# A transformer block on one core: the score steps of each head group start at 0.24 instead of 0.27 of the group's columns

## The chip, the cores and the metric

The kernel runs on one core of one Trainium2 chip. The core has TensorE (PE, matrix products), VectorE (DVE), ScalarE (ACT), GpSimd (POOL) and SyncE (SP, which here only issues DMAs). Each works through a queue of its own in order and waits on semaphores. The metric is the device time of one execution in microseconds.

## The reference

Eight sequences of 512 rows by 512 columns in float32 go through two layers, which makes 16 passes of attention and then an expert layer.

```python
x = L0_attn_x                                            # (8, 512, 512)
x = x + layernorm(attn(layernorm(x), w_qkv, w_o))        # 16 heads of 32, rotary, causal, T = 512
x = x + layernorm(ffn(layernorm(x), ...))

def attn(x, w_qkv, w_o):
    q, k, v = split(x @ w_qkv)                           # q and k rotated over all 32 columns of a head
    scores = where(causal, q @ k.T / sqrt(32), -inf)
    return (softmax(scores) @ v) @ w_o

def ffn(x, ...):
    h = x + attention(rmsnorm(x), ...)                   # 16 heads; q and k from latents of 128 columns,
                                                         # only half of each head's 32 columns is rotated
    return h + moe(rmsnorm(h), ...)                      # one shared and 7 routed experts, top 2, silu
```

## The kernel before

The program has two halves that run one after the other: `attention_layers` and `expert_layer`. The change touches only the order of work in the first.

**Cores and groups.** The attention half calls one attention pass over one sequence a core (a name of the program, not of the chip). There are 16 of them: `core_of` gives two sequences their first layer, then the same two their second, and so on. A core has four head groups of four heads each, so there are 64 groups, numbered 0 to 63; group n belongs to core n // 4. The pattern repeats every 16 groups.

**Softmax in two passes.** For group n the kernel makes the scores twice. The first time (step `S`, product at L1008, tile `score`) only to find each row's maximum: VectorE reads the scores with a mask and reduces them (`maxima`, L827). A head has three score steps: two products of 256 columns in one bank, then one of 384, then one of 512. The maxima are then transposed (step `M`, L1019), negated by ScalarE and sent by a small DMA into the stacks of q and k. The second time (step `ST`, L1031, tile `scoresT`) the maximum is subtracted inside the product, and ScalarE takes the exponential (L646). GpSimd cuts the diagonal blocks (L568) and adds column blocks up (L579, steps `A`); TensorE multiplies by V (step `PV`, L1045) and sums the rows (step `SM`, L1054).

**Rings.** `score` has 2 banks: a score step waits until VectorE has released the step two before it. `scoresT` has 2 banks, released by ScalarE. `middle` has 2 banks for everything else (projections, transposes, output products).

**What runs beside what.** During group n TensorE makes the second scores of group n, the first scores (`S`) of group n + 1, and transposes q and k of group n + 2 (step `T`, L980, just before `M`). Between these it takes projections and other products from a list: projections of q and k (`P`, L938 or L941; `KR`, L956; `KU`, L968), latents (`LAT`, L919), values (`V`, L989 or L993), and output products of the core before (`Y`, L1066). VectorE rotates q and k (L767 to L771, L787), inverts the sums in four pieces (step `I`, L840), and does the statistics of the layer norms (L741, L743, and L865 for the sum before one). GpSimd adds the rotated part (L558, L562) and takes the roots. `T` waits for that addition.

**What sets the order.** `head_group` gives each step of a group a share of the group's columns, and `merged` walks the sorted list: before a step with share s, filler steps are issued until s times all the columns of the group have gone by. `columns_of` is the weight of a step. The same list drives all engines: each engine walks it and does its own part of every step, so a step that moves on TensorE moves on VectorE, ScalarE, GpSimd and SyncE too. The score steps get their shares from one pair of numbers:

```python
steps += [(S_AT[0] + S_AT[1] * (3 * h + part), ("S", n + 1, h, part)) for h in range(GH) for part in range(3)]
```

and the second scores, which they are woven with, have their shares written out (first share of a column block, distance between heads):

```python
for j, (first, apart) in enumerate(((0.08, 0.03), (0.22, 0.04), (0.42, 0.03), (0.58, 0.03))):
    steps += [(first + apart * h, ("ST", n, j, h)) for h in range(GH)]
steps += [(share, ("PV", n, j)) for j, share in enumerate((0.37, 0.55, 0.74))]
```

Of the kernel before, what the change touches and what calls it, by code (L numbers as in the profile page):

```python
# [47 lines left out]
ST_BANKS = 2  # L48
QUARTERED = ("P", "KR", "KU", "V", "Y", "LAT")
T_AT = (0.9, 0.9, 0.9, 0.9)  # L50
S_AT = (0.27, 0.055)
WIDE = CT * FF
CHUNKS = 3 * WIDE // 512
CHUNKS_IN = {0: (0, 1), 1: (2, 3), 2: (4, 5)}
# [161 lines left out]
def head_group(n, groups):  # L216
# [6 lines left out]
    if n + 1 < groups:  # L223
        steps += [(S_AT[0] + S_AT[1] * (3 * h + part), ("S", n + 1, h, part)) for h in range(GH) for part in range(3)]
    for j, (first, apart) in enumerate(((0.08, 0.03), (0.22, 0.04), (0.42, 0.03), (0.58, 0.03))):
# [1983 lines left out]
```

How the kernel before makes its waits and increments, by code:

```python
                def load_weights():  # L404
# [3 lines left out]
                    sp.dma_start(rope2[:, :, :, :], tables[1]).then_inc(rest_in, 16)  # L408
                    sp.dma_start(ln1w[:, :], ln1_w).then_inc(rest_in, 16)
                    sp.dma_start(wlat[:, :, 0, :], kv_d.rearrange(by_c, p=P)).then_inc(rest_in, 16)
                    sp.dma_start(wlat[:, :, 1, :], q_d.rearrange(by_c, p=P)).then_inc(rest_in, 16)
                    sp.dma_start(wku[:, :], k_u).then_inc(rest_in, 16)
                    sp.dma_start(wvu[:, :], v_u).then_inc(rest_in, 16)
                    sp.dma_start(wq2[:, :, 0, :], q_u.rearrange("p (h d) -> p h d", h=NH)).then_inc(rest_in, 16)
                    sp.dma_start(wq2[:, :, 1, :], rope_q.rearrange("p (h d) -> p h d", h=NH)).then_inc(rest_in, 16)
                    sp.dma_start(wkr[:, :, :], rope_k.rearrange(by_c, p=P)).then_inc(rest_in, 16)
                    sp.dma_start(wo[:, 1], o_w.rearrange(by_c, p=P)).then_inc(rest_in, 16)
                    sp.wait_ge(consts, N_CONSTS)
# [1 line left out]
                def stack(n):  # L420
                    sp.wait_ge(high_done, 2 * (n + 1))
                    sp.wait_ge(*middle.out(("qT", n)))
                    sp.wait_ge(*middle.out(("kT", n)))
                    if n >= STACKS:
                        sp.wait_ge(st_filled, GH * TT * (n - STACKS + 1))
                    for h in range(GH):
                        for s, chosen in enumerate((slice(0, 2), slice(2, 0, -1), slice(0, 4, 3))):
```

## Time and profile before

| | |
|---|---|
| three runs | 2479.03, 2483.03, 2485.9 us; median 2483.03 |
| profiled execution | 2483.03 us, span of its instructions 2480.9 us |
| TensorE busy | 2207.7 us, 89% |
| VectorE busy | 1513.4 us, 61% |
| ScalarE busy | 1091.5 us, 44% |
| GpSimd busy | 1061.7 us, 43% |
| mean granted TensorE clock | 0.955 |

The span runs from the first instruction to the last. The attention half ends at about 1707 us. A busy share is a mean over stages; which engine is waited for differs from one kind of group to the next.

### The profile page before, as it was taken

How to read it: one execution, taken by the hardware profiler on the slowest of the kernel's cores; microseconds unless marked ns; L12 is line 12 of the kernel's file. 1: busy time of each engine (PE TensorE's matmuls, PEld its weight loads, DVE VectorE, ACT ScalarE, POOL GpSimd, SP SyncE). 2: the span in 40 equal slices, each digit the busy share in tenths (PEclk: the TensorE clock that was granted, in tenths of full speed). 3: DMA queues.
4: the chain of work that ended last, by engine and by line, in shares of the span. 5: the costliest groups of instructions: out<-in, count | busy, mean ns of one | idle time of the engine just before them, and what ended most of it. 6: DMA issues, size and time to landing. Idle time of an engine off the chain costs nothing. (4 is left out here: it accounts for less than half of the span.)

```text
span 2480.9 us, 38185 instructions
## 1 busy us (share of the span) xinstructions
PE 2207.7 (89%) x12960; PEld 1514.6 (61%) x12960; DVE 1513.4 (61%) x4196; ACT 1091.5 (44%) x2218; POOL 1061.7 (43%) x1092
## 2 busy tenths in 40 slices
PE   6898989999889999998999989896675899999984
PEld 5665555666556566564566755552454788888873
DVE  3666766656676675666757566663554556556556
ACT  1335554334545433455443345542422455555533
POOL 1455554535554445546353465543244133333312
PEclk9999999999999999999999999997787999999996
DMA  5443554434445454354554434442456588788766
GB/s 175 111 120 113 136 169 130 137 103 127 130 131 160 124 142 137 103 145 120 153 180 129 120 103 126 109 119 78 178 211 221 178 216 192 191 215 191 210 206 220
DMA packets 221918, 375.87 MB, mean 152 GB/s; under 512 B 24862, under 2 KB 95390, under 8 KB 218910
## 3 DMA queue, kind: packets, MB, share of 16 engines
q1 hardware_dynamic: 157982, 273.74, 37.6%
q0 software_dynamic: 17792, 39.99, 8.2%
q10 hardware_dynamic: 45952, 59.71, 6.7%
q8 instruction: 105, 1.72, 0.3%
q14 instruction: 87, 0.71, 0.1%
HBM read 126.88 MB, written 145.29 MB: 110 GB/s over the span
## 5 line engine op out<-in xcount | busy, mean ns | idle before, releaser
L646 ACT ACTIVATE probs<-scoresT 128x512 f32<-128x512 f32 (+3 forms) x1024 | 426.2, 437 | 513.4 <-PE scoresT L1031 499.5
L827 DVE CUSTOM_DVE_ANT_0 unused<-score,mask 128x128 bf16<-128x128 f32 (+3 forms) x1024 | 468.9, 486 | 272.0 <-PE score L1008 257.9
L1031 PE MATMUL scoresT<-stacks 97*128 97x256 f32 (+2 forms) x1024 | 421.7, 430 | 21.4 <-ACT probs L646 9.1
L1008 PE MATMUL score<-stacks 96*128 96x256 f32 (+2 forms) x1024 | 391.6, 428 | 36.5 <-DVE rowmax L827 35.6
L579 POOL TENSOR_TENSOR probs<-probs 128x1536 f32<-128x1536 f32 (+1 forms) x128 | 372.8, 2913 | 29.5 <-PE out_ps L1045 20.7
L1008 PEld LDWEIGHTS score<-stacks 96*128 96x128 f32 x1024 | 182.4, 191 | 201.7 <-issue 150.6
L840 DVE RECIPROCAL total<-total 128x128 f32<-128x128 f32 x256 | 232.6, 932 | 93.8 <-ACT whole L657 88.5
L568 POOL TENSOR_SCALAR_AFFINE_SELECT probs<-probs 128x512 f32<-128x512 f32 x256 | 164.5, 643 | 283.9 <-ACT probs L646 283.9
L1031 PEld LDWEIGHTS scoresT<-stacks 97*128 97x128 f32 x1024 | 190.5, 191 | 149.7 <-ACT probs L646 89.1
L938 PE MATMUL middle<-wqkv,XT 128*128 128x128 f32 x2048 | 268.1, 278 | 7.0 <-ACT XT L613 6.1
L1654 POOL DMA_INDIRECT h_summed<-y,goal x88 | 141.9, 1613 | 307.1 <-ACT y L1750 287.0
L938 PEld LDWEIGHTS middle<-wqkv,XT 128*128 128x128 f32 x2048 | 258.2, 194 | 17.3 <-ACT XT L613 6.6
L1066 PE MATMUL middle<-wo,outT 128*128 128x512 f32 x512 | 257.9, 598 | 0.0
L2059 PE MATMUL into<-xh,wh 128*128 128x512 f32 x480 | 202.8, 422 | 14.3 <-DVE wl L1804 7.6
L1045 PE MATMUL out_ps<-probs,V 128*32 128x512 f32 (+3 forms) x2048 | 196.3, 456 | 3.4 <-POOL probs L568 3.4
L558 POOL TENSOR_TENSOR qk<-qk,turned 128x512 f32<-128x512 f32 x64 | 81.4, 1272 | 268.5 <-DVE turned L771 268.5
L2059 PE MATMUL into<-xl,wh 128*128 128x512 f32 x480 | 193.8, 404 | 0.0
L2059 PE MATMUL into<-xh,wl 128*128 128x512 f32 x480 | 193.4, 403 | 0.0
L1966 DVE SCALAR_TENSOR_TENSOR acts<-acts,into 128x512 f32<-128x512 f32 x60 | 41.2, 687 | 179.0 <-ACT acts L1757 104.9
L767 DVE TENSOR_TENSOR qk<-middle,rope 128x512 f32<-128x512 f32 (+1 forms) x128 | 70.9, 554 | 125.6 <-PE middle L938 76.3
L562 POOL TENSOR_TENSOR qk<-qk,turned 128x256 f32<-128x256 f32 x64 | 48.3, 758 | 205.7 <-DVE turned L771 205.7
L622 ACT ACTIVATE parts<-middle 128x512 fp32r<-128x512 f32 x128 | 73.7, 596 | 140.1 <-PE middle L980 137.8
(181 smaller groups left out, 3809.5 us busy)
## 6 DMA issues: line engine op xcount, KB each, us to landing
stacks<-parts SPq DMA_DIRECT2D x768, 128.0 KB, 2.4
x_slots<-mask ACTq DMA_DIRECT2D x56, 1032.0 KB, 4.8
xr<-x_slots SPq DMA_DIRECT2D x22, 1032.0 KB
raw<-in_gates SPq DMA_DIRECT2D x24, 512.0 KB
raw<-in_ups SPq DMA_DIRECT2D x24, 512.0 KB
raw<-in_downs SPq DMA_DIRECT2D x24, 512.0 KB
normed<-in_L_attn_x SPq DMA_DIRECT2D x8, 1024.0 KB, 8.9
rows<-in_L_attn_x SPq DMA_DIRECT2D x8, 1024.0 KB, 5.7
```

The lines of the kernel that those rows point to most:

```text
L568: pool.affine_select(out=diagonal, in_=diagonal, compare_op=ALU.is_ge, fill=0.0, base=0, pattern=[[0, GH], [1, P]], channel_multiplier=-1)\
L579: pool.tensor_tensor(probs[0][:, :, P * j:T], probs[0][:, :, P * j:T], probs[j][:, :, :], ALU.add)\
L646: act.activation(probs[j][:, h, 0:width], scoresT[:, u % ST_BANKS, first:first + width], ACT.Exp, scale=SCALE).then_inc(exp_done, 1)
L827: ins = dve.tensor_tensor_reduce(unused[:, t, 0:width], score.bank(name)[:, first:first + width], mask[:, T - width:T], 1.0, MASKED, ALU.a ...
L840: dve.reciprocal(total[:, mine], total[:, mine]).then_inc(inverted, 1)
L938: ins = pe.matmul(to, tile_of(xT, c, t), wqkv[:, c, first:first + P], start=(c == 0), stop=(c == CT - 1))
L1008: ins = pe.matmul(score.bank(name)[:, first:first + width], heads[0:ROWMAX, 0, h, t * P:(t + 1) * P], heads[0:ROWMAX, 1, h, 0:width], star ...
L1031: pe.matmul(scoresT[:, u % ST_BANKS, 0:T - first], heads[0:ROWMAX + 1, 1, h, j * P:(j + 1) * P], heads[0:ROWMAX + 1, 0, h, first:T], start ...
L1045: ins = pe.matmul(out_ps[h * HD:(h + 1) * HD, P * j:T], v[:, c % 2, j, head:head + HD], probs[j][:, h, :], start=(j == 0), stop=(j == TT - 1))
L1066: ins = pe.matmul(middle.bank(name), tile_of(outT, (NG * f + c) % OUTS, t), wo[:, core_of(f)[1], c, :], start=(c == 0), stop=(c == CT - 1))
L1654: pool.indirect_dma_start(out=summed, out_offset=bass.IndirectOffsetOnAxis(ap=goal[:, k % XR, t:t + 1], axis=0), in_=y[:, k % GIVEN, t, :] ...
L2059: ins = pe.matmul(to, left, right, start=(first and n == 0), stop=(last and n == len(pairs) - 1))
```

## The change

```diff
--- before.py
+++ after.py
@@ -48,7 +48,7 @@
 ST_BANKS = 2
 QUARTERED = ("P", "KR", "KU", "V", "Y", "LAT")
 T_AT = (0.9, 0.9, 0.9, 0.9)
-S_AT = (0.27, 0.055)
+S_AT = (0.24, 0.055)
 WIDE = CT * FF
```

The first score step of a group gets the share 0.24 instead of 0.27, the last 0.845 instead of 0.875; the distance between them stays. No instruction is added, removed or changed in form. What the engines execute comes in another order in all groups but the last, which has no score steps in it.

TensorE in group 22, the third group of a first-layer core, in which the latents of the second-layer core behind it are made (L919), from the first head's score steps (L1008) to the second head's. Before:

```order
L1008 MATMUL score<-stacks1 128x256 x2
L919 MATMUL middle<-XT,wlat 128x512
L1031 MATMUL scoresT<-stacks0 128x384
L1008 MATMUL score<-stacks1 128x384
L1031 MATMUL scoresT<-stacks0 128x384
L919 MATMUL middle<-XT,wlat 128x512
L1045 MATMUL out_ps<-probs0,V 32x512 x4
L1008 MATMUL score<-stacks1 128x512
L1031 MATMUL scoresT<-stacks0 128x256
L1008 MATMUL score<-stacks1 128x256 x2
L1031 MATMUL scoresT<-stacks0 128x256
```

After:

```order
L1008 MATMUL score<-stacks1 128x256 x2
L1031 MATMUL scoresT<-stacks0 128x384
L919 MATMUL middle<-XT,wlat 128x512
L1008 MATMUL score<-stacks1 128x384
L1031 MATMUL scoresT<-stacks0 128x384 x2
L1008 MATMUL score<-stacks1 128x512
L919 MATMUL middle<-XT,wlat 128x512
L1045 MATMUL out_ps<-probs0,V 32x512 x4
L1008 MATMUL score<-stacks1 128x256 x2
L1031 MATMUL scoresT<-stacks0 128x256 x2
```

The first head's 512-column score stood behind the four products of `PV` (L1045). It now stands in front of the latent product and of these four, directly behind the second scores (L1031).

TensorE in group 21, the second group of a first-layer core, where the projections are L938. Before:

```order
L1008 MATMUL score<-stacks0 128x256 x2
L1031 MATMUL scoresT<-stacks1 128x384
L1008 MATMUL score<-stacks0 128x384
L1031 MATMUL scoresT<-stacks1 128x384
L938 MATMUL middle<-wqkv,XT 128x128 x4
L1045 MATMUL out_ps<-probs0,V 32x512 x4
L1008 MATMUL score<-stacks0 128x512
L1031 MATMUL scoresT<-stacks1 128x256
L1008 MATMUL score<-stacks0 128x256 x2
```

After:

```order
L1008 MATMUL score<-stacks0 128x256 x2
L1031 MATMUL scoresT<-stacks1 128x384
L1008 MATMUL score<-stacks0 128x384
L1031 MATMUL scoresT<-stacks1 128x384 x2
L1008 MATMUL score<-stacks0 128x512
L938 MATMUL middle<-wqkv,XT 128x128 x4
L1045 MATMUL out_ps<-probs0,V 32x512 x4
L1008 MATMUL score<-stacks0 128x256 x2
```

Here too the 512-column score of the first head moves in front of a projection and of the four products of `PV`.

TensorE at the end of group 23, a short group, in which the values are made (L993). Before:

```order
L1008 MATMUL score<-stacks0 128x512
L1045 MATMUL out_ps<-probs2,V 32x256 x4
L1008 MATMUL score<-stacks0 128x256 x2
L993 MATMUL middle<-wvu,latT 128x128
L1008 MATMUL score<-stacks0 128x384
L1008 MATMUL score<-stacks0 128x512
L980 MATMUL middle<-ident,qk 128x128 x8
L1019 MATMUL score<-ident,rowmax 16x128
```

After:

```order
L1008 MATMUL score<-stacks0 128x512
L993 MATMUL middle<-wvu,latT 128x128 x2
L1008 MATMUL score<-stacks0 128x256 x2
L1045 MATMUL out_ps<-probs2,V 32x256 x4
L1008 MATMUL score<-stacks0 128x384
L993 MATMUL middle<-wvu,latT 128x128
L1008 MATMUL score<-stacks0 128x512
L980 MATMUL middle<-ident,qk 128x128 x8
L1019 MATMUL score<-ident,rowmax 16x128
```

The last head's two 256-column scores move in front of the four products of `PV`, and its 384-column score in front of a value product. The last 512-column score keeps its place in front of the transposes of q and k (L980) and of the maxima (L1019).

## Rows read from the trace of the kernel before

**Rows 1.** Windows of busy time, attention half: stretch, length, busy per engine (instructions), clock, DMA share, GB/s.
```profile
0.00:1707.30 1707.30, 1559.99 (x10017) 1009.73 (x10017) 1084.82 (x3190) 750.53 (x1647) 824.12 (x874) 0.98 0.46 130
```

**Rows 2.** Waits of TensorE in the attention half: total, times, longest.
```profile
PE score L1008 <- DVE rowmax L827: 35.6, 41, 3.0
PE middle L980 <- POOL qk L558: 26.6, 9, 3.9
...
PE score L1019 <- DVE rowmax L827: 6.8, 6, 1.8
```

**Rows 3.** Timeline of TensorE, group 22: start, duration, engine, line, operation [idle before].
```profile
651.38 0.34 PE L1031 MATMUL scoresT<-stacks 97*128 97x384 f32 x1
651.56 1.02 PE L919 MATMUL middle<-XT,wlat 128*128 128x512 f32 x2
...
653.50 0.50 PE L1008 MATMUL score<-stacks 96*128 96x512 f32 x1
653.84 0.28 PE L1031 MATMUL scoresT<-stacks 97*128 97x256 f32 x1
```

**Rows 4.** Timeline of VectorE, first head's second maximum in groups 22 and 26.
```profile
651.99 0.42 DVE L827 CUSTOM_DVE_ANT_0 unused<-score,mask 128x256 bf16<-128x256 f32 x1
...
753.03 0.42 DVE L827 CUSTOM_DVE_ANT_0 unused<-score,mask 128x256 bf16<-128x256 f32 x1
```

**Rows 5.** Timeline of group 21 around its first output products, TensorE and VectorE.
```profile
619.31 0.37 PE L1031 MATMUL scoresT<-stacks 97*128 97x384 f32 x1
620.50 1.06 PE L1045 MATMUL out_ps<-probs,V 128*32 128x512 f32 x8
...
619.61 0.42 DVE L827 CUSTOM_DVE_ANT_0 unused<-score,mask 128x256 bf16<-128x256 f32 x1
```

**Rows 6.** Group 21: window of GpSimd's chain, then TensorE's timeline at its end.
```profile
621.69:637.25 15.56, 10.97 (x81) 8.18 (x80) 13.08 (x39) 4.65 (x11) 14.72 (x17) 1.00 0.36 136
...
637.36 0.65 PE L980 MATMUL middle<-ident,qk 128*128 128x128 f32 x4 [3.88 <-POOL qk L558]
...
638.59 2.36 PE L1054 MATMUL sum_ps<-probs,ones 128*32 128x512 f32 x16
```

**Rows 7.** Timeline of TensorE, group 28, the first head's 512-column score.
```profile
802.34 0.50 PE L1008 MATMUL score<-stacks 96*128 96x512 f32 x1 [1.19 <-DVE rowmax L827]
```

**Rows 8.** Timeline at the end of groups 23 and 29, TensorE and VectorE.
```profile
682.92 0.51 PE L1008 MATMUL score<-stacks 96*128 96x256 f32 x2
684.16 0.51 PE L1008 MATMUL score<-stacks 96*128 96x512 f32 x1 [0.33 <-DVE rowmax L827]
...
683.68 0.42 DVE L827 CUSTOM_DVE_ANT_0 unused<-score,mask 128x256 bf16<-128x256 f32 x1
...
832.53 0.68 DVE L827 CUSTOM_DVE_ANT_0 unused<-score,mask 128x512 bf16<-128x512 f32 x1
...
834.19 0.50 PE L1008 MATMUL score<-stacks 96*128 96x512 f32 x1 [0.48 <-DVE rowmax L827]
```

**Rows 9.** Timeline from group 24 to 25, TensorE and ScalarE.
```profile
714.00 0.27 PE L1019 MATMUL score<-ident,rowmax 128*16 128x128 f32 x1 [1.02 <-DVE rowmax L827]
...
714.44 1.26 PE L1054 MATMUL sum_ps<-probs,ones 128*32 128x512 f32 x16
...
718.08 0.50 PE L1031 MATMUL scoresT<-stacks 97*128 97x512 f32 x1 [0.46 <-DMA stacks<-negmax]
...
713.51 0.80 ACT L673 ACTIVATE normed<-normed,shift,rstd 128x512 f32<-128x512 f32 x1
714.37 0.27 ACT L630 ACTIVATE negmax<-score 16x128 fp32r<-16x128 f32 x1
```

**Rows 10.** Timeline of group 25, VectorE and GpSimd at the second sum.
```profile
733.12 2.08 DVE L865 TENSOR_TENSOR rows<-normed,rows 128x512 f32<-128x512 f32 x1
...
732.30 2.34 POOL L579 TENSOR_TENSOR probs<-probs 128x1024 f32<-128x1024 f32 x1
```

**Rows 11.** Window behind TensorE's wait in group 21.
```profile
637.80:641.20 3.40, 3.40 (x29) 1.33 (x28) 0.69 (x1) 1.57 (x4) 0.00 (x0) 0.51 0.08 18
```

## The prediction, on record before the changed kernel ran

> **What bounds the kernel now.** I read the windows of busy time first. The attention half, 1707.3 of 2480.9 us, has TensorE busy for 1559.99 us at a granted clock of 0.98 [rows 1]. So TensorE's queue is the bound there, and a new order of the same instructions can win only what TensorE now waits, and lose what it begins to wait. The expert half has its own order, which the edit doesn't touch. Second come TensorE's waits in the attention half: 35.6 us in 41 waits for row maxima to leave a score bank, 6.8 us for the last maxima before they are transposed, 26.6 us in 9 waits for rotated keys [rows 2]. Third, the timeline: groups 16 to 63 repeat, with period 16, the pattern of groups 0 to 15 but for the ends, and I worked each of the 16 kinds through once. Below, "group 22" stands for all of its kind.
>
> The score tile has two banks. A score step (two 256-column products, or one of 384, or one of 512 columns) may be issued when VectorE has read the step two before it. The third step of the first head (I call it the third score) therefore waits for the first score's two maxima.
>
> **The change.** No instruction is added or removed. The 12 score steps of a group move earlier by 0.03 of the group's columns, which in TensorE's queue is 0 to 1.7 us. What matters is what each is moved past.
>
> (a) *The latent groups, 8 of them (6, 10, 22, 26 and so on).* The third score moves in front of a latent product and of the four output products [order rows of group 22]. In group 22 TensorE comes to that place at 651.56; the score is now issued at 653.50 [rows 3]. The maxima that it waits for start at 651.99 and take 0.42, so they end at 652.41 [rows 4]; VectorE does them behind the rotated keys, whose place the edit leaves alone. TensorE, which waits for nothing here today, will stand from 651.56 to about 652.47, 0.9 us. Behind it nothing gives this back: the later waits of the group (for the latents' copies, for the keys) hang on TensorE's own products and move along. In group 26 the maxima end at 753.45 in the same pattern [rows 4]. 8 x 0.9 = +7.2 us.
>
> (b) *Groups 5, 21, 37, 53.* The same move, past one projection and the output products. TensorE issues the score before it at 619.31 and would be ready at 619.5; the maxima end at 619.61 + 0.42 = 620.03 [rows 5]. The stall is 0.6 us, and the output products, now at 620.50, start at about 621.4: 0.33 for the moved score and 0.6 for the wait, 0.9 us late. They release GpSimd's first addition of probabilities. GpSimd is then busy for 14.72 of 15.56 us until the keys are rotated, and TensorE waits 3.88 us for that at 637.36 [rows 6]. So this wait can take from 0.45 (if only the lag of TensorE arrives; a multiply on GpSimd now stretched beside VectorE may shrink) to 0.9 us more. I take 0.6: 4 x 0.6 = +2.4 us.
>
> (c) *Small delays.* In groups 12, 28, 44 the third score already waits 1.19 us [rows 7]; the maxima that it waits for move ahead of a rotation on VectorE and come sooner, but it stands 1.7 us sooner itself, and the next head's score then waits for maxima behind that rotation. No row gives the net; between the 1.19 us won and as much lost I take +0.2 each, since one wait takes the other's place. In groups 0, 16, 32, 48 the second head's 384-column score comes 1 us earlier and meets its bank 0.25 us too early. Together 3 x 0.2 + 4 x 0.25 = +1.6 us; below, zero for both.
>
> (d) *Groups that end on maxima.* In the eight short groups (7, 11, 23, 27 and so on) the last 512-column score waits 0.33 us beyond its weights, until the maxima that start at 683.68 and take 0.42 have ended [rows 8]. Those maxima belong to the score at 682.92, which moves in front of the output products, 0.43 us earlier; the last score, the transposed maxima and the rest of the group follow. 8 x 0.43 = -3.4 us. In groups 13, 29, 45, 61 the same wait is 0.48 us [rows 8], but VectorE first has a 512-column maximum until 832.53 + 0.68 = 833.21; with 0.64 for the two maxima behind it the bank is free at 833.85, and the last score comes at 833.91 instead of 834.19: 4 x 0.28 = -1.1 us.
>
> (e) *Costed at nothing.* In groups 8, 24, 40, 56 the last score moves in front of a projection whose statistics VectorE now does first, and the wait of 1.02 us at 714.00 goes [rows 9]. Late next is ScalarE: it copies until 714.31 before it takes the maxima at 714.37, and the product at 718.08, which needs them back by DMA, waits already (0.46 us). TensorE will wait there what it no longer waits at 714.00. If that cover is not there, 4 x 1.02 = 4.1 us are won. In group 25 VectorE is the bound over the last 13 us, and the same maxima and sums stand before the last score in either order. Two of its sums, the second taking 2.08 us beside a GpSimd addition of 2.34 us [rows 10], trade places with maxima; I take zero of -1.4 to +0.7 us each. In the other 30 or so groups the moved scores find their bank free: the order gives margins of 0.1 us and more.
>
> The Trainium skill, "SBUF — State Buffer", section on the shared port pair, says that VectorE with two SBUF inputs and GpSimd lock each other out for a whole instruction rather than sharing. The 2.08 us row, which ends after the addition has ended, agrees with it. By that rule the sum in group 25 would end when the addition ends wherever it is put, so the maxima moved in front of it would be free, and the sum of all terms would be up to 4 x 0.7 = 2.8 us lower. I don't count it, since the addition itself is released by output products that come later.
>
> **The sum.** +7.2 + 2.4 + 1.6 - 3.4 - 1.1 = +6.7 us on the profiled run, whose own time is 2483.03 us (span 2480.9 and 2.1 around it); this is also the median of the three runs, which spread over 6.9 us. I predict 2489.5 us, 0.26% slower. Within this case the terms' bounds give 2484 to 2494.
>
> **Rivals.**
> 1. *GpSimd's chain carries more.* All of (b) at its upper bound, and in groups 9, 25, 41, 57 the late output products move GpSimd's roots, ScalarE's normalised rows and so the next group's first transposes by 0.6 us. For it: GpSimd is busy 14.72 of 15.56 us [rows 6]. Against it: behind group 25 the copies of the transposes follow the sums and not the rows. 4 x 0.3 + 4 x 0.6 more: 2493 us.
> 2. *The stalls are given back.* The small reorderings win (ScalarE's ring of two banks gets a score between its second and third product of the last column block, 0.1 to 0.2 us in some 20 groups), the copies absorb (b), and half of (a) remains: 2484 us, no change that can be measured.
> 3. *Faster.* The change does what an earlier start would suggest: the 6.8 us for the last maxima go, the term (d) doubles, and the 35.6 us of waits for score banks lose a third, above all in group 25, where single waits reach 3.0 us [rows 2]. 6.8 + 4.5 + 12 less the 7.2 of (a): 16 us, 2467 us. Against it: in group 25 VectorE itself is full, and in 24 ScalarE is late next. It decides if the maxima of group 25 come a microsecond sooner.
> 4. *The clock.* After the wait of 3.88 us the granted clock is at 0.51 from 637.8 to 641.2, that is 1.2 instead of 2.4 GHz, and the sums at 638.59 take 2.36 us [rows 6, 11]; the same 16 take 1.26 at full clock [rows 9]. If the new stall of 0.9 us in the latent groups, where the clock is full now, brings it down, each costs 1.1 to 1.7 us more: 8 x 1.4 = 11, so 2500 us. Against it: waits of 1.02 and 1.19 us [rows 7, 9] stand in stretches at full clock. The Trainium skill, "TensorE: Matmul & The Clock Gate", part 1, has an idle array fall to half rate and a busy one return; by it only the long waits of (b) matter, where one more step of half clock would add some 1.7 us each, to 2496 us. The rows agree as far as they go.
>
> **Chances.** The forecast 0.45, rival 1 0.22, rival 2 0.17, rival 3 0.11, rival 4 0.05. A difference of 0.3%, 7.4 us, is about what a measurement of this kernel tells from no change: the bound lies at 2490.5, just above my value. A third of the forecast's case lies beyond it, with rivals 1 and 4: slower 0.42. Faster 0.10, from rival 3. The same 0.48. The range for 8 in 10 is 2477 to 2497 us: it takes in rivals 1 and 2 and leaves out 3 and 4.
>
> **What would show it.** (a): in the latent groups a wait of about 0.9 us for row maxima in front of the 512-column score, where there is none now; the total of that wait rises from 35.6 us by some 7 us, less (d). (b): the waits for rotated keys grow from 3.9 to about 4.5 us each, with the output products 0.9 us later. (d): groups 23 and 29 shorter by 0.4 and 0.3 us, group 22 longer by 0.9. (e): the wait for the last maxima gone in group 24, and the wait for the DMA of the maxima behind it at 1.5 us. The prediction is wrong if group 22 keeps its 28.4 us, or if group 24 with 25 gets more than 1 us shorter.

## The result, and the profile after

The changed kernel takes 2503.68 us (median of 6 runs, 2495.40 to 2510.86) against 2482.65 us for the kernel before (6 runs, 2479.03 to 2490.17). The ratio is 1.0081, 95% interval 1.0054 to 1.0107: slower by about 20 us. The forecast was 2489.5 us with a range of 2477 to 2497. The direction with the second largest chance came true, by three times the size of the sum. The profiled execution took 2508.09 us, its span 2505.9.

The page of the changed kernel begins:

```profile
span 2505.9 us, 38185 instructions
...
PE 2216.5 (88%) x12960; PEld 1520.3 (61%) x12960; DVE 1516.8 (61%) x4196; ACT 1082.9 (43%) x2218; POOL 1061.0 (42%) x1092
```

The waits of TensorE in its attention half (total, times, longest), against [rows 2]:

```profile
PE score L1008 <- DVE rowmax L827: 48.0, 51, 3.0
PE middle L980 <- POOL qk L558: 26.9, 9, 4.0
...
PE scoresT L1031 <- DMA stacks<-negmax: 10.6, 11, 3.8
```

and the wait for the last maxima over the whole span, which was 6.8 us in 6 waits:

```profile
PE score L1019 <- DVE rowmax L827: 1.1, 1, 1.1
```

The wait for score banks grew by 12.4 us, where I had forecast about 7 us more, less what (d) takes off. By kinds of group (explained below) it went from 1.4 to 10.7 us in kind 1, where I had forecast none, and from 0 to 6.0 us in the latent groups of (a). The wait for the last maxima is all but gone; I had forecast that the four waits of 1.02 us in (e) would go. The keys' wait did not grow in total.

The totals of a page don't say where. I therefore took the length of each of the 64 groups, from its first instruction on TensorE to the next group's first, out of each trace, and summed the differences from the kernel before by kind (kind k are the groups with n % 16 = k; four of each). The first column of numbers is what the prediction gave each; "again" is a second execution of the kernel before, the noise of the method; the other columns are the experiments below. The row of kinds 0 and 12 takes in what stands ahead of group 0. A last digit depends on where exactly a group is taken to begin, by up to 0.3 us in a sum.

| kinds | predicted | changed | again | E2 | E3 | E4 | E5 | E6 | E9 | E10 |
|---|---|---|---|---|---|---|---|---|---|---|
| 1 | 0 | **+14.0** | +2.5 | 0.0 | +14.5 | 0.0 | +2.1 | -1.9 | -2.9 | -2.7 |
| 6, 10 (a) | +7.2 | +8.1 | -0.1 | -0.4 | -0.5 | +7.9 | -0.1 | +0.4 | +7.4 | -0.2 |
| 5 (b) | +2.4 | +4.8 | +0.9 | -0.9 | +0.5 | -0.6 | +3.3 | -0.2 | +2.8 | +0.5 |
| 9 | 0 | **+6.4** | +0.8 | +2.3 | -0.5 | -1.1 | +7.3 | +3.3 | +7.6 | +1.9 |
| 8 (e) | 0 | **-3.7** | +0.2 | -3.7 | -0.1 | -0.1 | +0.2 | -3.7 | -3.7 | -3.8 |
| 7, 11, 13 (d) | -4.5 | -4.2 | -1.0 | -4.9 | 0.0 | -0.2 | -0.1 | -5.2 | -5.3 | -5.4 |
| 0, 12 (c) | +1.6 | +0.9 | 0.0 | +0.6 | +0.2 | +1.6 | +1.4 | +0.9 | +1.0 | +2.6 |
| 2, 3, 4, 14, 15 | 0 | +2.7 | +0.5 | +4.2 | -0.4 | +0.6 | -0.1 | +9.2 | +7.4 | +1.0 |
| attention half | +6.7 | +29.0 | +3.7 | -2.8 | +13.7 | +8.2 | +14.0 | +2.8 | +14.3 | -6.1 |

The attention half grew by 29 us. The expert half, which the edit doesn't touch, was about 4 us shorter in this execution, so the span grew by 25. Between the two executions of one and the same kernel before it differs more than that (span less the end of group 63: 773.6 and 763.9 us), so it tells nothing of the change.

The second execution of the kernel before has a longer attention half than the first, by 3.7 us. Taken from the second, the last row reads +25.3 for the changed kernel, -6.5 (E2), +10.0 (E3), +4.5 (E4), +10.3 (E5), -0.9 (E6), +10.6 (E9) and -9.8 (E10). The timed differences are +21.0, -4.5, +12.1, +3.3, +5.7, -0.5, +11.8 and -9.4: within 2.1 us of these, but for the changed kernel and E5, which lie over 4 us below. So the sums of the table run a few microseconds high, above all in kind 1.

**The missed term.** In group 33 VectorE now does this (start, duration, engine, line, operation):

```profile
937.41 0.49 DVE L827 CUSTOM_DVE_ANT_0 unused<-score,mask 128x384 bf16<-128x384 f32 x1
937.83 0.08 DVE L827 DVE_READ_ACCUMULATOR2_ANT rowmax<- 128x1 f32 x1
937.83 4.25 DVE L752 TENSOR_SCALAR normed<-normed,meanvar,rstd 128x512 f32<-128x512 f32 x2
942.00 0.68 DVE L827 CUSTOM_DVE_ANT_0 unused<-score,mask 128x512 bf16<-128x512 f32 x1
```

GpSimd at the same time, and then TensorE:

```profile
938.36 3.43 POOL L579 TENSOR_TENSOR probs<-probs 128x1536 f32<-128x1536 f32 x1 [0.33 <-PE out_ps L1045]
```

```profile
942.74 0.56 PE L1008 MATMUL score<-stacks 96*128 96x384 f32 x1 [2.95 <-DVE rowmax L827]
943.09 0.42 PE L1031 MATMUL scoresT<-stacks 97*128 97x256 f32 x1
943.30 1.91 PE L1066 MATMUL middle<-wo,outT 128*128 128x512 f32 x2
```

The same pair and the same addition in the kernel before, VectorE and then GpSimd:

```profile
928.26 1.22 DVE L752 TENSOR_SCALAR normed<-normed,meanvar,rstd 128x512 f32<-128x512 f32 x2
929.40 0.54 DVE L827 CUSTOM_DVE_ANT_0 unused<-score,mask 128x384 bf16<-128x384 f32 x1
```

```profile
929.63 3.47 POOL L579 TENSOR_TENSOR probs<-probs 128x1536 f32<-128x1536 f32 x1 [0.43 <-PE out_ps L1045]
```

L752 is the normalising step `LN` of the next core's rows; two pairs of them stand in groups 1, 17, 33 and 49. (Two stand in groups 13, 29 and 45 as well. No meeting shows there: the two that come nearest to the addition take 0.45 and 0.54 us before and after.) Before, the second pair was through 0.15 us ahead of GpSimd's first addition of probabilities. The edit put the pair behind the first head's 384-column maxima, and it put `PV`, whose end releases the addition, 0.41 us earlier, since a `Y` product moved behind `PV`. The addition now starts at 938.36, and the second of the pair ends at 942.08, 0.3 us after the addition. The addition itself is not slowed: 3.43 us here, 3.47 before. The maxima behind it are late, and TensorE stands 2.95 us beyond its weights before the second head's 384-column score. After this wait the clock is at half in group 33, 1.2 GHz; window of the changed kernel (stretch, length, busy times, clock, DMA share, GB/s):

```profile
942.90:946.30 3.40, 3.40 (x10) 1.62 (x14) 1.88 (x6) 0.77 (x2) 0.68 (x2) 0.50 0.00 0
```

where the kernel before had full clock from the same place in the group on:

```profile
933.50:943.00 9.50, 7.22 (x65) 6.07 (x67) 5.77 (x20) 1.83 (x6) 5.66 (x5) 1.00 0.60 221
```

Group 17 grew by 2.6 us, groups 33 and 49 by 5.8 and 5.6. The wait of 2.95 us is the same in all three, and group 49 has half clock around it too. In group 17 the clock stays full behind it:

```profile
521.10:533.20 12.10, 9.82 (x75) 7.46 (x75) 7.95 (x29) 2.26 (x7) 5.24 (x5) 1.00 0.47 174
```

E3 repeats this, with full clock behind the wait in group 17 and half clock in 33 and 49. So the meeting costs its wait each time, and half clock on top of it in some groups.

**Where the half clock is.** A stretch at granted clock c has 2 x (1 - c) of its length at half clock. Summed over the groups, from the clocks of the traces before rounding, kind 1 went from 8.8 to 20.6 us at half clock, kind 9 from 27.3 to 43.7, and all other kinds together from 46.9 to 46.3. In the second execution of the kernel before it is 14.2, 29.9 and 51.3. An estimate from these numbers: 28 us more at half clock cost at most 14 of the 29 us.

### The profile page after: what moved, and what is told of

Read it like the earlier page. It is cut to its first block and busy times, and to the rows that moved or that the text cites. A ratio compares the mean times of both kernels' runs of the same rounds, so it can differ in the third digit from the quotient of the medians.

```text
span 2505.9 us, 38185 instructions
## 1 busy us (share of the span) xinstructions
PE 2216.5 (88%) x12960; PEld 1520.3 (61%) x12960; DVE 1516.8 (61%) x4196; ACT 1082.9 (43%) x2218; POOL 1061.0 (42%) x1092
## 5 line engine op out<-in xcount | busy, mean ns | idle before, releaser
L646 ACT ACTIVATE probs<-scoresT 128x512 f32<-128x512 f32 (+3 forms) x1024 | 417.2, 436 | 554.8 <-PE scoresT L1031 550.1
L1008 PE MATMUL score<-stacks 96*128 96x256 f32 (+2 forms) x1024 | 390.1, 424 | 50.1 <-DVE rowmax L827 48.0
L1031 PE MATMUL scoresT<-stacks 97*128 97x256 f32 (+2 forms) x1024 | 405.9, 431 | 23.3 <-DMA stacks<-negmax 10.6
L1008 PEld LDWEIGHTS score<-stacks 96*128 96x128 f32 x1024 | 182.1, 193 | 250.3 <-issue 178.7
L938 PE MATMUL middle<-wqkv,XT 128*128 128x128 f32 x2048 | 269.5, 279 | 7.0 <-ACT XT L613 6.1
L938 PEld LDWEIGHTS middle<-wqkv,XT 128*128 128x128 f32 x2048 | 259.9, 194 | 21.9 <-issue 8.4
L1031 PEld LDWEIGHTS scoresT<-stacks 97*128 97x128 f32 x1024 | 187.9, 193 | 128.2 <-ACT probs L646 71.9
L2059 PE MATMUL into<-xh,wh 128*128 128x512 f32 x480 | 202.3, 421 | 14.5 <-DVE wl L1804 7.6
L1045 PE MATMUL out_ps<-probs,V 128*32 128x512 f32 (+3 forms) x2048 | 199.5, 463 | 5.8 <-POOL probs L568 5.6
```

Source lines behind the costliest of these rows:

```text
L646: act.activation(probs[j][:, h, 0:width], scoresT[:, u % ST_BANKS, first:first + width], ACT.Exp, scale=SCALE).then_inc(exp_done, 1)
L938: ins = pe.matmul(to, tile_of(xT, c, t), wqkv[:, c, first:first + P], start=(c == 0), stop=(c == CT - 1))
L1008: ins = pe.matmul(score.bank(name)[:, first:first + width], heads[0:ROWMAX, 0, h, t * P:(t + 1) * P], heads[0:ROWMAX, 1, h, 0:width], star ...
L1031: pe.matmul(scoresT[:, u % ST_BANKS, 0:T - first], heads[0:ROWMAX + 1, 1, h, j * P:(j + 1) * P], heads[0:ROWMAX + 1, 0, h, first:T], start ...
L1045: ins = pe.matmul(out_ps[h * HD:(h + 1) * HD, P * j:T], v[:, c % 2, j, head:head + HD], probs[j][:, h, :], start=(j == 0), stop=(j == TT - 1))
L2059: ins = pe.matmul(to, left, right, start=(first and n == 0), stop=(last and n == len(pairs) - 1))
```

## The experiments

Each experiment ran beside the kernel before on the same chip. The median of the kernel before was 2484.1, 2476.8 and 2476.6 us in the three sets of runs, so only ratios and differences are compared. The changed kernel stands at +21.0 us. Changed lines shift the line numbers, by one at most (L751 or L753 for L752) and by seven in E7.

**E1. The pair of normalising steps earlier.** The changed kernel with

```diff
-            steps[7:7] = [("LN", p, 2), ("LN", p, 3)]
+            steps[6:6] = [("LN", p, 2), ("LN", p, 3)]
```

> The changed kernel, with the second pair of normalising steps (LN p 2, LN p 3) two places earlier in the list of group kind 1 (groups 17, 33, 49), so that VectorE does them before any maxima of the next group. Theory A (collision): in these groups the pair of L752 (1.22 us before, 4.25 us after) has come to stand beside GpSimd's first addition (3.4 us) and waits for it; then its maxima are late and TensorE stands 3.5 us. With the pair done earlier, groups 17, 33, 49 return to their length before within 0.5 us: 12 to 14 us less than the changed kernel, about 2491 us. Theory B (score banks or clock): the groups are longer because the scores meet full banks or the clock falls, the pair is a bystander: it takes 1.2 us and nothing else changes, 2503 us.

Measured: 2500.55 against 2484.13 us, ratio 1.0060 (1.0042 to 1.0078), +16.4: less than 5 us given back, not 12 to 14. Theory A is right in part. Groups 17, 33 and 49 went from +14.0 to +4.7 us together, and the wait of 2.95 us is gone. But the pair now stands ahead of the first head's first maxima, VectorE and TensorE in group 33:

```profile
931.81 1.46 DVE L752 TENSOR_SCALAR normed<-normed,meanvar,rstd 128x512 f32<-128x512 f32 x2
...
933.19 0.28 DVE L827 CUSTOM_DVE_ANT_0 unused<-score,mask 128x128 bf16<-128x128 f32 x1
```

```profile
933.87 0.50 PE L1008 MATMUL score<-stacks 96*128 96x512 f32 x1 [1.30 <-DVE rowmax L827]
```

The third score waits for those maxima, 1.30 us beyond its weights. This is the wait of (a), made longer by what stands in VectorE's queue. And in group 1, which I had not thought of, the same edit makes the meeting longer: the pair takes 4.17 us there, TensorE waits 3.82 us instead of 1.83, and the group is 1.3 us longer than in the changed kernel. (This edit, and those of E9, E10 and E12, also move normalising steps in groups 13, 29 and 45. Those groups keep their length within 0.3 us by it.)

**E9. All four normalising steps together**, where VectorE waits for TensorE anyway. The changed kernel with

```diff
-            steps[3:3] = [("LN", p, 0), ("LN", p, 1)]
-            steps[7:7] = [("LN", p, 2), ("LN", p, 3)]
+            steps[3:3] = [("LN", p, t) for t in range(TT)]
```

> The changed kernel, with all four normalising steps of group kind 1 together (at the place where two stand now), so VectorE has them behind it, in time in which it waits for TensorE anyway. Theory A (the pair costs by what stands behind it, first 3.5 us by GpSimd's addition, in e1_norms_first 1.9 us by its own 1.2 us in front of the first score's maxima): no pair stands ahead of maxima that TensorE waits for, groups 17, 33, 49 come within 0.5 us of their length before, the attention half ends about 14 us earlier than in the changed kernel and 5 us earlier than in e1_norms_first; 2491 us. Theory B (there is another wait in these groups that takes over): each keeps 1 us or more, 2496 us or above.

Measured: 2488.66 against 2476.82 us, ratio 1.0046 (1.0029 to 1.0063), +11.8. Groups 17, 33 and 49 are at -1.0, +1.5 and +0.6 us, the attention half 14.7 us shorter than in the changed kernel, as theory A has it. The timed gain is 9 us, where it has 12. The groups keep to it within the noise of 1.6 us that the second execution of the kernel before shows for this kind. Group 1 is 4 us shorter, which I had not expected; E12 accounts for most of it.

**E7. Is it a lock?** The changed kernel with GpSimd's addition in two halves, in groups 17, 33 and 49:

```diff
+                    half = GH // 2
+                    if n in (17, 33, 49) and j == 1:
+                        pool.tensor_tensor(probs[0][:, :half, P * j:T], probs[0][:, :half, P * j:T], probs[j][:, :half, :], ALU.add)
+                        pool.tensor_tensor(probs[0][:, half:, P * j:T], probs[0][:, half:, P * j:T], probs[j][:, half:, :], ALU.add)\
+                            .then_inc(added, 1)
+                        return
```

> The changed kernel, with GpSimd's first addition (128x1536) of groups 17, 33, 49 issued as two of half the size (768 columns each); nothing else moves. Theory A (VectorE and GpSimd lock each other out for a whole instruction): the second L752 gets in between the two halves, the pair takes 2.4 to 3.0 us instead of 4.25, TensorE waits 1.7 to 2.1 us instead of 3.5 us: 3 x 1.6 = 5 us less, 2499 us. Theory B (both slow down in proportion while they overlap, or the pair waits for something else that ends at the same time): the pair stays at 4.0 us or more, 2503 us.

VectorE, GpSimd and TensorE in group 33:

```profile
931.20 2.62 DVE L759 TENSOR_SCALAR normed<-normed,meanvar,rstd 128x512 f32<-128x512 f32 x2
933.74 0.68 DVE L834 CUSTOM_DVE_ANT_0 unused<-score,mask 128x512 bf16<-128x512 f32 x1
```

```profile
931.72 1.81 POOL L581 TENSOR_TENSOR probs<-probs 128x768 f32<-128x768 f32 x1 [0.32 <-PE out_ps L1052]
933.49 1.99 POOL L583 TENSOR_TENSOR probs<-probs 128x768 f32<-128x768 f32 x1
```

```profile
934.48 0.44 PE L1015 MATMUL score<-stacks 96*128 96x384 f32 x1 [1.33 <-DVE rowmax L834]
...
934.88 1.02 PE L1073 MATMUL middle<-wo,outT 128*128 128x512 f32 x2
```

The pair takes 2.62 us instead of 4.25 and ends 0.3 us after the first half, 1.7 us before the second half ends, so it doesn't wait for the addition's result. The wait is 1.33 instead of 2.95 us, 1.6 less, as a lock for a whole instruction says; sharing would have left the pair as it was. The next output products take 1.02 us instead of 1.91: after 1.33 us of waiting the clock here stays at 2.4 GHz. Groups 17, 33 and 49 fell from +14.0 to +5.5 us together; of these 8.6 us the three shorter waits are 4.9. The rest I put down to the clock: the three have 6.6 us at half clock instead of 15.7, and half of that difference is 4.5 us. Ratio 1.0050 (1.0030 to 1.0069): 8 us less than the changed kernel, where I had expected 5, since I left the clock out.

**E12. The same in the kernel before**: all four together (the diff of E9), with 0.27.

> The kernel before, with all four normalising steps of group kind 1 together and nothing else. Theory A: group 1 loses its wait of 1.7 us and some of the half clock behind it, -3 to -4 us; groups 17, 33, 49, where the pair takes 1.2 us already, within 0.5 us: 3 us less than before. Theory B (in group 1 it is the clock alone): all within 0.5 us.

Measured: 2473.88 against 2476.60 us, ratio 0.9985 (0.9976 to 0.9995), group 1 shorter by 2.4 us and the other three of its kind within the noise: theory A, at the low end. With the order of before in group 1, four other executions (the second of the kernel before, E2, E4 and E5) are 0.5 us longer there at most, so the 2.4 us are more than noise. In the kernel before group 1 has the collision already, VectorE, GpSimd and TensorE:

```profile
97.80 3.37 DVE L752 TENSOR_SCALAR normed<-normed,meanvar,rstd 128x512 f32<-128x512 f32 x2
```

```profile
95.99 3.47 POOL L579 TENSOR_TENSOR probs<-probs 128x1536 f32<-128x1536 f32 x1
```

```profile
101.83 0.60 PE L1008 MATMUL score<-stacks 96*128 96x384 f32 x1 [1.45 <-DVE rowmax L827]
102.22 1.91 PE L938 MATMUL middle<-wqkv,XT 128*128 128x128 f32 x8
```

and in E12 the four take 2.14 us, and this score has no wait (the two 256-column scores ahead of it now have one, of 0.6 us):

```profile
90.99 2.14 DVE L751 TENSOR_SCALAR normed<-normed,meanvar,rstd 128x512 f32<-128x512 f32 x4
```

```profile
100.64 0.34 PE L1007 MATMUL score<-stacks 96*128 96x384 f32 x1
100.82 1.05 PE L937 MATMUL middle<-wqkv,XT 128*128 128x128 f32 x8
```

The row of 3.37 us stood in the trace that I predicted from.

**E2 to E5. The change in some kinds of group only**, each the kernel before with another set:

```diff
+SOONER = (7, 8, 11, 13)   # E2; E3 (1,); E4 (6, 10); E5 (5, 9)
-        steps += [(S_AT[0] + S_AT[1] * (3 * h + part), ("S", n + 1, h, part)) for h in range(GH) for part in range(3)]
+        steps += [((0.24 if n % 16 in SOONER else S_AT[0]) + S_AT[1] * (3 * h + part), ("S", n + 1, h, part))
+                  for h in range(GH) for part in range(3)]
```

> The kernel before, with 0.24 for the scores in the groups n with n % 16 in (7, 8, 11, 13) only (where the changed kernel was shorter), 0.27 in all others. Theory A: the difference of the two kernels is a sum over groups that do not act on each other: -3.0 (7, 11), -1.3 (13), -3.7 (8): 2475 us, and each of these groups shows its own part. Theory B: a gain in one group is given back in the next, since a queue other than TensorE's is late: 2483 us.

> The kernel before, with 0.24 in the groups n % 16 = 1 only (1, 17, 33, 49). Theory A: +14 us alone, 2497 us, with the pair of L752 at about 4.2 us in groups 17, 33, 49 and a wait of 3.5 us for row maxima; group 1 unchanged. Of it 9 us are the wait and the rest half clock behind it. Theory B (it takes the accumulated lag of the groups ahead, or the clock's phase): at most +3 us.

> The kernel before, with 0.24 in the latent groups n % 16 in (6, 10) only. Theory A: the stall in front of the third score, 0.9 to 1.2 us in each of 8 groups, +8 us: 2491 us. Theory B (given back behind it): +0 to +4 us.

> The kernel before, with 0.24 in the groups n % 16 in (5, 9) only. Theory A (parts add up): kind 5 alone +4.8 us; of kind 9's +6.4 us in the changed kernel 2.4 us came from group kind 8 (e2_gainers shows them without any edit in 9), so here +4.0; together +8.8 us, 2492 us. Theory B: in kinds 5 and 9 the wait for GpSimd's keys takes the delay in: +3 us or less, 2487 us.

Measured ratios: E2 0.9984 (0.9969 to 1.0000), -4.5 us; E3 1.0040 (1.0019 to 1.0061), +12.1; E4 1.0016 (1.0003 to 1.0029), +3.3; E5 1.0024 (1.0011 to 1.0037), +5.7. Their sum, +16.6, lies in the changed kernel's interval. By the groups that each edits the parts add up closely (table): kind 1 alone gives +14.5, the latent kinds +7.9, kinds 7, 11, 13 -4.9 and kind 8 -3.7. E3 is theory A. E4's timed loss is less than its own groups say (its interval ends at 7.2 us): by them it is theory A, by the time theory B. E5's is less too (10.6 by the groups of kinds 5 and 9, 8.8 expected by theory A). Against the second execution of the kernel before E4's attention half comes to +4.5, near its time, since other kinds are shorter by chance; for E5 a gap stays open. E2 won 4.5 of the 8 us expected: kind 9, which it doesn't touch, is 2.3 us longer behind a shorter kind 8. Here theory B is right.

In E5 kind 9 alone costs 7.3 us. The third score waits there too, in group 57:

```profile
1567.56 0.50 PE L1009 MATMUL score<-stacks 96*128 96x512 f32 x1 [1.08 <-DVE rowmax L828]
```

and the first output products, behind it, come 1.2 to 1.6 us later in the four groups. What this costs by the group's end swings from 0.2 to 3.7 us between groups and executions, with the wait itself 1.07 or 1.08 us each time. The swing goes with the clock. Groups 9 and 25 of the changed kernel, which are 3.5 and 0.2 us longer than before:

```profile
298.58:327.83 29.25, 22.97 (x110) 11.99 (x106) 21.18 (x56) 13.23 (x29) 18.45 (x34) 0.78 0.43 127
723.77:749.92 26.15, 19.51 (x110) 10.64 (x106) 20.27 (x56) 13.24 (x29) 18.76 (x34) 0.87 0.48 142
```

All four groups of the kernel before have 0.87 as well, 6.8 us at half clock. Over the changed kernel, E1, E5, E7 and E9, the seven groups of this kind that keep 6.8 us are 0.2 to 0.7 us longer than before, and the thirteen with 9 to 17 us are 0.8 to 3.7 us longer. What decides between the two is not settled. In E6, where the third score no longer waits, groups 25 and 57 have the longer half clock too.

**E6. One step of the twelve.** The changed kernel, with the third score alone at its former share:

```diff
-        steps += [(S_AT[0] + S_AT[1] * (3 * h + part), ("S", n + 1, h, part)) for h in range(GH) for part in range(3)]
+        steps += [(S_AT[0] + S_AT[1] * (3 * h + part) + (0.03 if (h, part) == (0, 2) else 0.0), ("S", n + 1, h, part))
+                  for h in range(GH) for part in range(3)]
```

> The changed kernel, but the third score of the first head at its former share (0.38 instead of 0.35), in all groups. Theory A (the loss in kinds 5, 6, 9 and 10 comes from this one step, which waits for the first score's maxima in front of the output products): kinds 6 and 10 back to +0.0 to +0.1 us each, kinds 5 and 9 to +0.3 us or less each; kind 1 stays longer, since the normalising pair still stands behind the 384-column maxima; together 15 us less than the changed kernel, 2488 us. Theory B (it is the whole group of twelve steps that comes too early): half of it at most, 2496 us or above.

Measured: 2476.07 against 2476.60 us, ratio 0.9998 (0.9988 to 1.0007), 12 us below theory A. Without this one step the rest of the change costs nothing in time: kinds 6 and 10 at +0.4, kind 5 at -0.2, and kind 9 at +3.3 (2.3 of which E2 has as well). It doesn't gain either, although kinds 7, 8, 11 and 13 do. Against them stand +9.2 in the row of small kinds: 0.57 in each group of kind 4, which only E6 has, and +2.3 in group 62, where 21.6 us are at half clock instead of 10.2. (E9 has the same in group 62; the changed kernel has 6.8 us at half clock there and is 1.4 us shorter.) I had expected kind 1 to stay longer, and it doesn't (-1.9). VectorE and GpSimd in group 33:

```profile
926.88 1.00 DVE L753 TENSOR_SCALAR normed<-normed,meanvar,rstd 128x512 f32<-128x512 f32 x2
```

```profile
927.84 3.48 POOL L580 TENSOR_TENSOR probs<-probs 128x1536 f32<-128x1536 f32 x1 [0.74 <-PE out_ps L1046]
```

The pair stands where it stands in the changed kernel, but with the third score behind the output products these come 0.42 us later, and the pair gets through just as the addition begins. So the collision needs both: the pair later and the addition earlier.

**E8. The other direction.** The kernel before with `S_AT = (0.30, 0.055)`.

> The kernel before with S_AT = (0.30, 0.055), the scores as much later as the change made them earlier. Theory A (what counts is which single step each crosses): no mirror image. Kinds 6 and 10 stay as before (the third score already stands behind the output products), kinds 7, 11, 13 lose what they won (+4 us), kind 8 is unchanged or a little longer: 2483 to 2492 us. Theory B (earlier scores are worse by themselves, so later ones are better): 2463 to 2475 us.

Measured: 2565.0 against 2476.82 us, ratio 1.0357 (1.0332 to 1.0381). Both theories fall. The waits of TensorE, and group 18 at its end, where `M` waited for nothing before:

```profile
PE score L1019 <- DVE rowmax L827: 82.6, 56, 3.2
```

```profile
578.58 0.48 PE L1008 MATMUL score<-stacks 96*128 96x512 f32 x1
579.07 0.66 PE L980 MATMUL middle<-ident,qk 128*128 128x128 f32 x4
581.01 0.27 PE L1019 MATMUL score<-ident,rowmax 128*16 128x128 f32 x1 [1.28 <-DVE rowmax L827]
```

The last score slipped behind the first transposes of `T`, so `M` has only half of `T` to wait behind. This wait alone is 75.8 of the 88 us. I had looked at the third score only, and not at the end of the group.

**Control.** The kernel before once more, one execution.

> The kernel before once more, for a second trace of it: how far do the groups of two executions of one kernel differ. Theory A: within 0.1 us in the groups without long waits, up to 1 us in kinds 1, 5, 9 and 12, where half clock follows a long wait; the expert half within 4 us. Theory B (the differences by group read so far are noise of one execution): several groups of kinds 6, 7, 8, 10 differ by 0.5 us or more.

2476.88 us. Theory A: kinds 6, 7, 8 and 10 differ by 0.3 us at most in any group, kind 1 by up to 1.6 (group 49), kind 12 by up to 1.0, the sum by 3.7. Terms below 1 us a kind with long waits (1, 5, 9, 12) are not told from noise here. Only the expert half differs by more than I expected, nearly 10 us.

**E10. The best of it.** The kernel before with the diff of E9 and `SOONER = (7, 8, 11, 13)`.

> The kernel before, with 0.24 in the groups n % 16 in (7, 8, 11, 13) and with all four normalising steps of group kind 1 together. Theory A (parts add up): -3 us from e2_gainers over the attention half and -3 to -4 us in group 1, where the pair of L752 takes 3.37 us in the kernel before as well, beside GpSimd's first addition: 6 to 7 us less than the kernel before, ratio 0.997. Theory B: the four normalising steps together push the rotated rows of the next projection back, 0 to 2 us less, ratio 0.999 or above.

Measured: 2467.21 against 2476.60 us, ratio 0.9962 (0.9949 to 0.9975), 9.4 us faster than the kernel before (theory A had 6 to 7), and faster than all others here. Its waits for score banks are below the 35.6 us of before:

```profile
PE score L1008 <- DVE rowmax L827: 30.3, 32, 3.0
```

## Why the prediction was wrong, step by step

**The step that failed** is the sentence at the end of (e), "In the other 30 or so groups the moved scores find their bank free: the order gives margins of 0.1 us and more". I asked of each moved score whether its own bank is free, at the durations of before. In groups 17, 33 and 49 it is VectorE's queue that changes: the pair of L752 trades places with maxima and meets GpSimd's addition. That is worth +14.0 us of the +22 that the sum lacks in the attention half. The second execution of the kernel before would make it 11.5, and the time of E3, which has the edit there alone, +12.1. E9 and E6 take it away, and E7 takes off 8.6 us. The sum had nothing for it. It had nothing for kind 9 either (+6.4), nor any half clock outside rival 4. (Its own terms give 2489.7 us; 2489.5 is what I put down.)

The Trainium skill, "SBUF — State Buffer", section "SBUF: two separate sides", states the lock: whichever of the two starts first holds the pair of ports for the whole instruction, and the other blocks. The page's condition covers VectorE operations in a 2-port mode as well as those with two SBUF inputs. The trace agrees for L752, an operation with one tensor input: 4.25 us for the pair beside an addition of 3.43, 2.62 us beside one of 1.81, 1.22 us without. In the prediction I told the rule with two inputs only, and applied it to one sum (L865), where it would have lowered the time. I did not list the other VectorE instructions which the edit moves relative to GpSimd's.

**(a) Right.** +8.1 us against +7.2. In group 22 the score waits 0.76 us beyond its weights, 0.95 us longer in the group; TensorE, VectorE:

```profile
658.69 1.02 PE L919 MATMUL middle<-XT,wlat 128*128 128x512 f32 x2
...
661.00 0.50 PE L1008 MATMUL score<-stacks 96*128 96x512 f32 x1 [0.76 <-DVE rowmax L827]
```

```profile
660.52 0.42 DVE L827 CUSTOM_DVE_ANT_0 unused<-score,mask 128x256 bf16<-128x256 f32 x1
```

**(b) The mechanism right, the size too small.** +4.8 us against +2.4 (noise 0.9). I had said that the wait for the keys would grow from 3.9 to 4.5 us. It is 3.76 to 4.03 us, and came later almost as a whole. TensorE in group 5; the first row is the third score, which now waits, and the output products behind it are 0.91 us late:

```profile
201.94 0.50 PE L1008 MATMUL score<-stacks 96*128 96x512 f32 x1 [0.38 <-DVE rowmax L827]
...
219.97 1.09 PE L980 MATMUL middle<-ident,qk 128*128 128x128 f32 x4 [3.76 <-POOL qk L558]
...
221.63 2.36 PE L1054 MATMUL sum_ps<-probs,ones 128*32 128x512 f32 x16
```

The transposes start 0.75 us later in each of the four groups than before, where I had taken 0.6 of a bound of 0.9. The groups are 1.2 us longer on average, and the remaining 0.4 is not told from noise: the transposes behind the wait take 1.09 us where those of [rows 6] took 0.65, so half clock has begun already, but in the kernel before it has begun by then in group 37, and in three of the four groups of its second execution.

**(d) right**, within the noise: -4.2 us against -4.5. **(c) not settled**: +0.9 us against +1.6, but single groups of it go from -2.3 (group 0) to +1.7 us (group 44), and groups 16, 32 and 48 are 0.2 to 0.7 us longer. In kinds 2, 3, 14 and 15 nearly each group is 0.2 to 0.6 us longer, which I had at zero: +2.7 us in the line of small kinds, with 1.4 us won in group 62.

**(e) Wrong: the cover was not there**, or only in part. Kind 8 wins 3.7 us, nearly its bound of 4.1. From VectorE, TensorE and ScalarE at the end of group 24:

```profile
720.14 0.69 DVE L827 CUSTOM_DVE_ANT_0 unused<-score,mask 128x512 bf16<-128x512 f32 x1 [0.53 <-PE score L1008]
```

```profile
722.14 0.27 PE L1019 MATMUL score<-ident,rowmax 128*16 128x128 f32 x1
...
725.69 0.50 PE L1031 MATMUL scoresT<-stacks 97*128 97x512 f32 x1
```

```profile
723.54 0.25 ACT L630 ACTIVATE negmax<-score 16x128 fp32r<-16x128 f32 x1
```

I had the product at L1031 wait 1.5 us for the small DMA. It doesn't wait at all in groups 8, 24 and 40, and 0.96 us in group 56. ScalarE is late next, as I said, but the DMA that follows was quicker in group 24; DMA issues before (size, median us from issue to landing), and after:

```profile
stacks<-negmax ACTq DMA_DIRECT2D x1, 8.0 KB, 3.4
```

```profile
stacks<-negmax ACTq DMA_DIRECT2D x1, 8.0 KB, 1.8
```

The change did not make it quick. In the kernel before this DMA takes 1.8 us in groups 8 and 40, where the product doesn't wait, and 3.4 and 3.0 us in groups 24 and 56. Its median over all 64 groups is 1.8 us. I had read group 24 and taken it for all of its kind. Of these 3.7 us, 2.3 come back as length of kind 9 (E2; 0.8 of it is in the second execution of the kernel before too). My own sign for (e) did not show: groups 24 and 25 together are 0.75 us shorter, not more than 1 us. Kind 9 itself (25 and its like) I had at zero for its end, and did not see that the third score moves ahead of the output products there as in (a) and (b), only without a latent product: +6.4 us together, E5 +7.3. By the clocks shown under E5 a large part of it is half clock.

**The rivals.** Rival 1 named kinds 5 and 9 as where GpSimd's chain carries more, and priced them at +3.6 and +2.4 us; they gave +4.8 and +6.4, but kind 9 by another way than its GpSimd chain alone: the third score's wait and the clock. Rival 2 fell: the stalls of (a) are not given back. Of rival 3 the first item came true, as the waits for the last maxima fell from 6.8 to 1.1 us; the others did not. Rival 4 came nearest in the total, 2500 us, by luck: the stalls of 0.9 us in the latent groups bring no half clock (group 22 grew by the stall alone), the half clock came in kinds 1 and 9.

## What to carry to other kernels

When an order table moves, compare each engine's new order and not only the moved instruction's own wait: list every VectorE instruction that changes sides with a long GpSimd one, and price the meeting at the whole length of the GpSimd instruction. Before pricing a cover from one group, read the same rows in all groups of its kind. Look for one place in the trace of before where the same line is slow; here it stood in group 1, at 3.37 instead of 1.22 us. And a share table is a set of crossings, not a dial: 0.03 earlier cost 0.8%, 0.03 later 3.6%, and a choice by kind of group (with the four normalising steps together) won 0.4%.

## What the runs showed of the hardware that I had not expected

- Between two GpSimd instructions back to back, the waiting VectorE instruction gets through: in E7 the second L752 ran from the end of the first half (933.5) to 933.8, and the second half took 1.99 instead of 1.81 us.
- The length of one wait doesn't tell whether half clock follows. The wait of 2.95 us is followed by it in groups 33 and 49 of the changed kernel (1.91 us for two products of 512 columns in group 33), not in group 17 (1.02 us). In group 1 a wait of 1.83 us is followed by it in the changed kernel, one of 1.80 us is not in E7. So in this kernel the same meeting made a group 2.6 to 5.8 us longer.
- An 8 KB DMA issued at the same place of four groups of one trace took 1.8 us in two of them and 3.0 and 3.4 us in the others. No run here shows why.
